# Moving the rotary and normalisation products of a random-feature attention from VectorE to GpSimd, with the three engines' head orders rotated by one head

## The reference

```python
def _softmax_kernel(x, R):
    n = jnp.sqrt(jnp.sum(x * x, axis=-1, keepdims=True))
    x = x / jnp.maximum(n, 1e-06)
    p = jnp.einsum('...d,ed->...e', x, R)
    feats = jnp.concatenate([jnp.sin(p), jnp.cos(p)], axis=-1)
    return feats / math.sqrt(F)
...
q = q * cos + _rotate_half(q) * sin
k = k * cos + _rotate_half(k) * sin
...
qp = _softmax_kernel(q, rand_matrix)
kp = _softmax_kernel(k, rand_matrix)
kv = jnp.einsum('bhsf,bhsd->bsfd', kp, v)
out = jnp.einsum('bhsf,bsfd->bhsd', qp, kv)
```

## Time and profile before

| | us |
|---|---|
| median of 3 timed runs | 7942.13 (7479.22 to 7977.28) |
| the profiled execution, own time | 7549.52 |
| its span, first to last instruction of the slowest core | 7548.1 |
| spans of the 8 cores in it | 7453.7 to 7548.1 |
| glue of stages 0 to 3 in it, with the projection under it | 388, 408, 409, 330 |
| everything after the attention stages (from 2190) | 5358 |

### The profile page before, as it was taken

One profiled execution on the slowest core, in us unless ns is written; L12 is line 12 of the kernel. 1 busy time (PEld: TensorE's weight loads), 2 busy tenths in 40 slices (PEclk: granted clock), 3 DMA queues, 4 the chain that ended last, 5 costly groups with the idle time before them and its releaser, 6 DMA issues.

```text
span 7548.1 us, 63284 instructions; the slowest of 8 cores (7453.7 to 7548.1 us)
## 1 busy us (share of the span) xinstructions
PE 5322.1 (71%) x23362; PEld 2315.3 (31%) x23362; DVE 1744.6 (23%) x2583; ACT 1411.5 (19%) x1675; POOL 561.5 (7%) x1064
## 2 busy tenths in 40 slices
PE   1364444344137599898989898539989898989891
PEld 1121111111013244343434343214434343434340
DVE  4325354454630000101010101230010101010114
ACT  4333534435341110000000000001010000000100
POOL 0000000000001011010101110001101010101010
PEclk9987677676558799999999999759999999989785
DMA  6652322323038544343434343324434343334342
GB/s 152 158 101 36 59 37 50 48 36 43 0 45 147 118 72 73 65 70 66 71 66 72 65 73 64 95 89 72 72 66 70 66 72 66 66 57 69 56 75 96
DMA packets 420666, 542.35 MB, mean 72 GB/s; under 512 B 251920, under 2 KB 268560, under 8 KB 412176
## 3 DMA queue, kind: packets, MB, share of 16 engines
q0 software_dynamic: 152640, 403.85, 32.1%
q1 hardware_dynamic: 267728, 134.46, 7.1%
HBM read 891.61 MB, written 50.33 MB: 125 GB/s over the span
## 4 chain that ended last, share of the span: by engine, by line
PE 65%; DVE 14%; ACT 10%; DMA 4%; issue 4%; SPq 2%; DVEq 1%; ACTq 0%; POOL 0%; POOLq 0%
PE pb L908 27%; PE pb L1003 27%; PE pb L591 4%; DVE nsq_b L525 4%; DVE mids L965 4%; PE pb L721 2%; ACT attn_st L654 2%; ACT L479 2%; PE pb L359 1%; DVE ot_b L1093 1%; SPq L691 1%; DMA wup_b<-wup 1%; ACT fk L491 1%; PE pb L1112 1%; SPq L666 1%
## 5 line engine op out<-in xcount | busy, mean ns | idle before, releaser
L908 PE MATMUL pb<-xn_tb,wup_b 128*128 128x512 bf16 x9216 | 2086.9, 391 | 71.3 <-DMA wup_b<-wup 71.2
L1003 PE MATMUL pb<-mids,wdn_b 128*128 128x512 bf16 x9216 | 2040.0, 385 | 110.1 <-DVE mids L965 109.3
L908 PEld LDWEIGHTS pb<-xn_tb,wup_b 128*128 128x128 bf16 x9216 | 921.6, 100 | 1235.9 <-issue 340.7
L1003 PEld LDWEIGHTS pb<-mids,wdn_b 128*128 128x128 bf16 x9216 | 912.1, 99 | 1238.1 <-issue 222.2
L965 DVE TENSOR_TENSOR mids<-mids,pb 128x4096 bf16<-128x4096 bf16 x64 | 282.9, 4421 | 2166.0 <-ACT mids L925 2159.9
L925 ACT ACTIVATE mids<-pb 128x512 bf16<-128x512 f32 x576 | 344.0, 597 | 1664.5 <-PE pb L908 1664.3
L578 PE MATMUL pb<-un_b,rt_sb 128*64 128x512 bf16 x96 | 58.1, 605 | 773.7 <-DVE un_b L529 773.7
L1025 DVE TENSOR_TENSOR acc_tb<-acc_tb,pb 128x512 f32<-128x512 f32 x320 | 219.9, 687 | 1500.2 <-PE pb L1003 1500.2
L591 PE MATMUL pb<-xn_st,wbuf 128*128 128x512 bf16 x1536 | 465.7, 473 | 55.4 <-DMA xn_st<-xn_scr 51.3
L983 POOL DMA_DIRECT2D wdn_b<-wdn x576 | 305.5, 544 | 1976.0 <-PE pb L1003 1593.7
L925 ACT ACT_TABLE_LOAD x12 | 15.4, 1283 | 2077.2 <-PE pb L908 2077.2
(11 more groups left out here) (102 smaller groups left out, 2501.5 us busy)
## 6 DMA issues: line engine op xcount, KB each, us to landing
wup_b<-wup POOLq DMA_DIRECT2D x288, 512.0 KB, 5.2
wdn_b<-wdn POOLq DMA_DIRECT2D x576, 256.0 KB, 5.0
wbuf<-wq POOLq DMA_DIRECT2D x64, 512.0 KB, 5.2
wbuf<-wo POOLq DMA_DIRECT2D x64, 512.0 KB, 6.0
x_tm<-x SPq DMA_DIRECT2D x16, 1024.0 KB, 7.7
x_tm<-xs SPq DMA_DIRECT2D x16, 1024.0 KB, 6.4
wbuf<-wk POOLq DMA_DIRECT2D x32, 512.0 KB, 5.2
wbuf<-wv POOLq DMA_DIRECT2D x32, 512.0 KB, 5.8
```

Source lines behind the costliest of these rows:

```text
L908: ins = t.matmul(pb[k % 2][:, 0:CH], wup_b[i % 2][:, kc * 128:(kc + 1) * 128], xn_tb[:, kc * TB + n * CH:kc * TB + (n + 1) * CH], start=(k ...
L1003: ins = t.matmul(pb[4 + idx % 2][:, 0:CH], wdn_b[(mc * EG + e3) % 6][:, dc * 128:(dc + 1) * 128], mids[:, e3 * DCN * TB + dc * TB + n * CH ...
```

## The change

The five bf16 products and sums of a head (L513, L515, L517, L519, L529) leave VectorE and are issued by GpSimd, on tiles of the same size and type, counted on a new semaphore `cP` (`PP = 5` for each head). VectorE keeps five instructions for a head (`NV = 5`). GpSimd's weight DMAs now stand in the same list: the first three ahead of head 0, then one behind each head's fifth instruction. Each GpSimd instruction waits for the one before it. TensorE's and ScalarE's lists are rotated: `nsq` of a head stands one round earlier relative to `phi`, and `phi` comes first in a round. Names and buffers stay as they were.

```diff
-    NV = 10
+    NV = 5
+    PP = 5
...
-        for hh in range(NHEADS + 2):
-            if hh >= 2:
-                k = hh - 2
-                t_ops.append(("nsq", k))
-                t_ops.append(("phi", k))
-                if nxt:
-                    t_ops.append(("qkv", k))
+        for hh in range(NHEADS + 3):
+            if hh >= 3:
+                t_ops.append(("phi", hh - 3))
+            if 1 <= hh <= NHEADS:
+                t_ops.append(("nsq", hh - 1))
+            if nxt and 2 <= hh < NHEADS + 2:
+                t_ops.append(("qkv", hh - 2))
             if hh < NHEADS:
                 t_ops.append(("pq", hh))
...
+            for hh in range(NHEADS):
...
+                wt(g, "G", "cS", S0 + Spos[("pqe", hh)])
+                if hh >= 4:
+                    wt(g, "G", "mT", T0 + Tpos[("nsq", hh - 4)])
+                wt(g, "G", "cP", cnt["cP"])
+                inc(g.tensor_mul(sb_[:], pq_sb[hh % 4][:], s_), "cP")
+                wt(g, "G", "cP", cnt["cP"])
+                inc(g.tensor_mul(qb[:], srcT[:, base:base + ST], c_), "cP")
+                wt(g, "G", "cP", cnt["cP"])
+                inc(g.tensor_add(qb[:], qb[:], sb_[:]), "cP")
+                wt(g, "G", "cP", cnt["cP"])
+                inc(g.tensor_mul(sb_[:], qb[:], qb[:]), "cP")
+                if hh >= 4:
+                    wt(g, "G", "mT", T0 + Tpos[("phi", hh - 4)])
+                wt(g, "G", "cV", gl_at(hh, 2))
+                wt(g, "G", "cP", cnt["cP"])
+                inc(g.tensor_mul(un_b[hh % 4][:], qb[:], invn_b[hh % 4][:]),
+                    "cP")
+                if nxt and 3 <= hh + 2 < NOC:
+                    dw(hh + 2)
...
         @blk.vector
...
             for hh in range(NHEADS):
...
-                inc(v.tensor_mul(sb_[:], pq_sb[hh % 4][:], s_), "cV")
...
-                inc(v.tensor_mul(qb[:], srcT[:, base:base + ST], c_), "cV")
...
-                inc(v.tensor_add(qb[:], qb[:], sb_[:]), "cV")
...
-                inc(v.tensor_mul(sb_[:], qb[:], qb[:]), "cV")
                 wt(v, "V", "cS", S0 + Spos[("sqrt", hh)])
                 wt(v, "V", "cV", cnt["cV"])
                 inc(v.tensor_scalar_max(nsq_b[hh % 4][:], nsq_b[hh % 4][:],
                                         1e-6), "cV")
                 wt(v, "V", "cV", cnt["cV"])
                 inc(v.reciprocal(invn_b[hh % 4][:], nsq_b[hh % 4][:]), "cV")
...
-                inc(v.tensor_mul(un_b[hh % 4][:], qb[:], invn_b[hh % 4][:]),
-                    "cV")
                 wt(v, "V", "mT", T0 + Tpos[("phi", hh)])
...
                 elif kind == "nsq":
-                    wt(t, "T", "cV", gl_at(k, 4))
+                    wt(t, "T", "cP", gp_at(k, 4))
...
                 elif kind == "phi":
-                    wt(t, "T", "cV", gl_at(k, 7))
+                    wt(t, "T", "cP", gp_at(k, 5))
```

More of the change, by code:

```diff
@@ L34 @@
 MASKV = 2.0 / 128.0
-SEM_NAMES = (["mT", "cV", "cS", "dCY", "dCG", "dsp", "dxt", "dgr", "dst",
+SEM_NAMES = (["mT", "cV", "cS", "cP", "dCY", "dCG", "dsp", "dxt", "dgr", "dst",
               "dxb", "dou", "dat", "dcc", "dwi0", "dwi1"]
@@ L412, in build_program @@
         s_ops = []
[L413 to L419, removed]
+        for hh in range(NHEADS + 3):
+            if 1 <= hh <= NHEADS:
+                s_ops.append(("sqrt", hh - 1))
+            if hh >= 3:
+                s_ops.append(("sin", hh - 3))
+            if nxt and 2 <= hh < NHEADS + 2:
+                s_ops.append(("evq", hh - 2))
             if hh < NHEADS:
@@ L426, in build_program @@
         C["Spos"] = Spos
+        C["P0"] = P0 = cnt["cP"]
         gl_at = lambda hh, k: G0 + NV * hh + k
+        gp_at = lambda hh, k: P0 + PP * hh + k
         C["glue_cV_end"] = G0 + NV * NHEADS
+        C["glue_cP_end"] = P0 + PP * NHEADS
         coV0 = G0 + NV * NHEADS
@@ L441, in build_program @@
             C["xn_ld"] = (f"dn{(st + 1) % 2}", cnt[f"dn{(st + 1) % 2}"])
[L443 to L456, removed]
+        wldn = []
@@ new lines, in build_program, with _, dw @@
+        C["wld"] = wldn
+        @blk.gpsimd
+        def _(g, st=st, nxt=nxt, T0=T0, S0=S0, Tpos=Tpos, Spos=Spos,
+              gl_at=gl_at, gp_at=gp_at, wldn=wldn):
+            c_ = cos_sb[:, st * ST:(st + 1) * ST]
+            s_ = sin_sb[:, st * ST:(st + 1) * ST]
+            def dw(j):
+                if j >= 3:
+                    wt(g, "G", "mT", qkvT_at(st + 1, j - 3))
+                else:
+                    wt(g, "G", "mT", qkvT_at(st, NOC - 1))
+                sname = f"dw{j % 3}"
+                inc(g.dma_start(out=wbuf[j % 3][:],
+                                in_=qkvsrc[j][0][qkvsrc[j][1]]), sname, 16)
+                wldn.append((sname, cnt[sname]))
+            if nxt:
+                for j in range(3):
+                    dw(j)
+            for hh in range(NHEADS):
+                isq = hh < H
+                srcT = (q_f if isq else k_f)[st % 2]
+                base = (hh if isq else hh - H) * ST
+                qb = qr_b[hh % 4]
+                sb_ = sq_b[hh % 4]
+                wt(g, "G", "cS", S0 + Spos[("pqe", hh)])
[17 more added lines that the diff above has]
+                    dw(hh + 2)
+            if nxt:
+                for j in range(NHEADS + 2, NOC):
+                    dw(j)
@@ L458, in _ @@
         @blk.scalar
         def _(s, st=st, nxt=nxt, T0=T0, S0=S0, Tpos=Tpos, Spos=Spos,
-              gl_at=gl_at, s_ops=s_ops):
+              gl_at=gl_at, gp_at=gp_at, s_ops=s_ops):
             if st >= 1:
@@ L463, in _ @@
                 wt(s, "S", "cV", caps[st - 1]["glue_cV_end"])
+                wt(s, "S", "cP", caps[st - 1]["glue_cP_end"])
             for op in s_ops:
@@ L468, in _ @@
                     if k >= 4:
-                        wt(s, "S", "cV", gl_at(k - 4, 1))
+                        wt(s, "S", "cP", gp_at(k - 4, 1))
                     wt(s, "S", "cS", cnt["cS"])
@@ L476, in _ @@
                     if k >= 4:
-                        wt(s, "S", "cV", gl_at(k - 4, 6))
+                        wt(s, "S", "cP", gp_at(k - 4, 5))
                     wt(s, "S", "cS", cnt["cS"])
@@ L500, in _ @@
         def _(v, st=st, T0=T0, S0=S0, Tpos=Tpos, Spos=Spos, gl_at=gl_at):
-            c_ = cos_sb[:, st * ST:(st + 1) * ST]
-            s_ = sin_sb[:, st * ST:(st + 1) * ST]
             for hh in range(NHEADS):
[L504 to L512, removed]
-                inc(v.tensor_mul(sb_[:], pq_sb[hh % 4][:], s_), "cV")
-                wt(v, "V", "cV", cnt["cV"])
-                inc(v.tensor_mul(qb[:], srcT[:, base:base + ST], c_), "cV")
-                wt(v, "V", "cV", cnt["cV"])
-                inc(v.tensor_add(qb[:], qb[:], sb_[:]), "cV")
-                wt(v, "V", "cV", cnt["cV"])
-                inc(v.tensor_mul(sb_[:], qb[:], qb[:]), "cV")
                 wt(v, "V", "cS", S0 + Spos[("sqrt", hh)])
@@ L525, in _ @@
                 inc(v.reciprocal(invn_b[hh % 4][:], nsq_b[hh % 4][:]), "cV")
-                if hh >= 4:
-                    wt(v, "V", "mT", T0 + Tpos[("phi", hh - 4)])
-                wt(v, "V", "cV", cnt["cV"])
-                inc(v.tensor_mul(un_b[hh % 4][:], qb[:], invn_b[hh % 4][:]),
-                    "cV")
                 wt(v, "V", "mT", T0 + Tpos[("phi", hh)])
@@ L547, in _ @@
         def _(t, st=st, nxt=nxt, T0=T0, S0=S0, Tpos=Tpos, Spos=Spos,
-              gl_at=gl_at, t_ops=t_ops, co_mT0=co_mT0, coV0=coV0, C=C):
+              gl_at=gl_at, gp_at=gp_at, t_ops=t_ops, co_mT0=co_mT0,
+              coV0=coV0, C=C):
             wt(t, "T", "dCG", cCG)
```

## The result

| | before | after |
|---|---|---|
| median, 10 timed runs each | 7777.81 (7479.22 to 7997.38) | 8077.38 (7872.62 to 8400.54) |
| profiled execution, own time | 7549.52 | 7888.15 |
| spans of its 8 cores | 7453.7 to 7548.1 | 7855.8 to 7887.1 |

The changed kernel is slower: the ratio after to before is 1.0536, 95% interval 1.047 to 1.0603.

A forecast was written before the change was run, and what follows sets the result against it. No engine is full; a head's chain handed from engine to engine bounds the attention glue. Stages 0 to 2 +315, stage 3 +13, stage ends -4 make +324 on the profiled 7549.5: 7875 us, range 7690 to 8330.

The forecast's parts named there:

- the qkv block: TensorE's matmuls (L591) between `nsq` and `pq` in stages 0 to 2, taken at 5.1 us a head.
- The ring: Closed chain from `nsq` to the next over TensorE, VectorE and GpSimd, nothing overlapping: 19.4 us a head, 14.0 in stage 3.
- its closing entry on VectorE: VectorE's list keeps the range reduction of head h ahead of maximum and reciprocal of head h+1.
- falling fast at first, so their mean is nearer the lower end: Step sizing the qkv block: five blocks in turn go from 6.28 down to 4.65 us, so 5.1 was taken.
- Rival B: TensorE's clock stays low for the whole qkv block, 6.9 us in place of 5.1: +119, total 7995; chance 0.14.
- s: Time of one of a head's five GpSimd products, gap included: taken as 1.2 us, bounded by 0.53 and 3.46.
- The ends of the stages: First heads of stages 0 and 3 lose about 4 us each, three stage ends gain 4 each: together -4 us.
- A: GpSimd nearly as quick as VectorE, s from 0.53 to 0.8 us; total 7580 at 0.53; chance 0.08.
- C: GpSimd products at s = 2.0 us, from bf16 conversion or dear completion: +352, total 8225; chance 0.13.
- D: VectorE's maximum not held behind the range reduction, so the ring avoids `phi`: 13.6 us a head, total 7470; chance 0.03.

The follow-up runs named there:

- the move alone: Kernel before, with only the five products put on GpSimd and TensorE's and ScalarE's lists unchanged: glue 1767 us (+112), lowest time 7576 us.
- the fastest kernel: Kernel before, with all three engines' lists rotated and the four rotary products on GpSimd, `un_b` staying on VectorE: ratio to before 0.9092.

## Why the prediction was right and wrong

**Right in the mechanism, wrong in two steps.** One term of the sum, the qkv block, was too small, and the sum was put on the wrong level, so that the number given said something else than the text. Both are below. The ring was read from the lists alone and is in the trace step for step: the maximum right behind the range reduction, VectorE idle for `phi`, TensorE idle for GpSimd. Undoing its closing entry on VectorE took 487 us off; taking the block out took 409 off.

**The sizes of the terms**, per head of stage 0:

| term | forecast | measured |
|---|---|---|
| `nsq` | 0.43 | 0.37 |
| qkv block | 5.1 | 6.03 |
| `pq` | 0.22 | 0.32 |
| `phi` to range reduction | 0.82 | 0.58 |
| range reduction | 2.18 | 2.19 |
| maximum and reciprocal | 3.99 | 4.08 |
| `un_b`, DMA, four products, hand-over | 6.67 | 6.90 |
| sum | 19.4 | 20.47 |

The term that was mis-sized is the block. The step that failed is "falling fast at first, so their mean is nearer the lower end": the earlier trace rows is right for the kernel before, but I carried its cycle over to a ring with 13 us of idle. There nearly all blocks are alike at 5.99. (In the kernel before the five blocks of that cycle are 6.17, 5.31, 4.87, 4.65 and 4.54 from start to start of what follows, a mean of 5.1.) Rival B had half of it: the clock is lower for most of the block, not for all of it. With 0.43 for a matmul at the lower level and 3.62 / 16 = 0.23 at the higher, 5.99 is some 12 of the 16 at the lower. The weight loads of the block shown above, one for each matmul, say the same: they come 0.43 apart as far as 653.37, and the last three stand close together.

```profile
652.94 0.15 PEld L611 LDWEIGHTS pb<-xn_st,wbuf 128*128 128x128 bf16 x1 [0.28 <-issue]
653.37 0.58 PEld L611 LDWEIGHTS pb<-xn_st,wbuf 128*128 128x128 bf16 x3 [0.28 <-issue]
```

With s at 1.29 to 1.31 instead of 1.2, the hand-over already in it, and the DMA at 0.42 instead of 0.53 the last line is 0.23 over. Over 66 intervals 1.04 more each is +69; stage 3, 14.53 for 14.0, is +12.

**The ends and the costs at nothing.** The ends of the stages came to about -1.5 us in all, where -4 was said, and by smaller terms that cancel: the first heads of stages 0 and 3 lost 1.7 and 1.6 us, not 4, and the three stage ends gave back 4.6 together, not 12. In stages 1 and 2 the first block still waits for `xn_st` (38.6 us in all on the page of the profile), which hides the slower first head. VectorE's 280 us of work taken away brought nothing, as said. "The two engines are never at work together in the ring, so I cost nothing for anything they might share" holds in the changed kernel, where none of VectorE's instructions for the 96 heads lies beside a GpSimd product, and would have failed in the move alone.

**The level.** The sum was +324, and the glue measures +404 to +406. The two profiled own times differ by 339, near the forecast, which is partly luck: the core profiled before had some 80 us in its feed-forward part that the core after had not. The step that failed here is "I keep the point at 7875 and let the range speak for that". It put a sum made on one execution (7549.5) below the median of the runs shown, 7942, so that the number reads as a kernel 0.8% faster, although the text and the chances said clearly slower, and slower it is, by 5.4%. Against the median shown, the same +324 is 8266. The measured median, 8077, lies 2.6% over the point and inside the range, and its own reference moved down to 7778 with more runs: it is 300 over that. A forecast of a ratio, 1.043 as worked out and 1.0536 measured, would have been free of this. That 8077 lies inside the range is no merit of the sum, since the range was made wide to hold this doubt among others.

**The rivals.** A: s is 1.3, far from 0.8. C: not 2.0 either. D: not in this kernel; made on purpose, its ring takes 13.83 against the 13.6 worked out, and the total 7394 against 7470.

## What to carry to other kernels

Where engines run fixed lists, write down for each instruction what stands ahead of it on its own engine as well as what it needs, and look for closed rings: rotating two lists of three made one that went through an unrelated 6 us block, and rotating the third as well was worth 487 us. A move to a slower engine costs what lies on the ring, not what the engines' busy times say: the same products were +112 in one order, +406 in another, and part of a kernel 9% faster in a third. State a forecast as a difference or a ratio first, and put it on the level of the median, not of one execution.

## What the runs showed of the hardware

- A GpSimd product of 128x512 bf16 takes 1.04 to 1.16 us and 1.29 to 1.31 from start to start where each waits for the one before, 2.5 times VectorE's 0.53. The Trainium skill's page "GPSIMD Engine Reference", section "Performance versus the Vector engine", gives about 2.6 cycles an element; at the 1.2 GHz by which the page reckons that is an estimate of 1.11 us for 512, and the trace agrees. Its measured ratio of 1.96 is for float32, and the bf16 products here do not follow it: 1.15 to 0.42 is 2.7.
- VectorE and GpSimd hold each other up, and it depends on the instruction and on who started first. When the second pass of the range reduction (float32, from SBUF to SBUF, 0.43 us) started during a GpSimd product, it ended 0.28 behind the end of that product: it took 1.38 when it started 0.06 behind the product's start (the move alone), and 0.68 when it started 0.75 behind (VectorE's list rotated). With 0.15 or less of the product left it kept its 0.43. The first and the third pass of the move alone, which read PSUM, kept 0.75 and 0.69 in all of more than 90 cases beside a product, and so did the reciprocal its 3.35 in the 84 cases of the fastest kernel. There GpSimd's products took up to 1.64 instead of 1.15, `un_b` itself up to 1.68 instead of 0.69, and some maxima 1.2. The Trainium skill's page "SBUF — State Buffer", section "Who interferes with whom", has an exclusive lock of a shared port pair: the pass that ends just behind the product is what that would give.
- The same 16 matmuls took 6.0 us where TensorE idled 13.4 us a head, 4.6 to 6.2 in a cycle of four where it idled 12.9, and mostly 3.6 in the fastest kernel, where it was busy for 101 of 153 us. The granted clock in the glue of stage 0 was 0.68 (after), 0.73 (before) and 0.91 (fastest). The idle time does not settle the length of a block: with VectorE's list rotated, heads of 13.8 us each had blocks that fell from 6.4 to 4.8 us over 18 heads and then stood at 6.4 again, while the idle time grew from 6.5 to 8. What decides it was not tried.

```profile
core 2: us, PE busy (x) PEld busy (x) DVE busy (x) ACT busy (x) POOL busy (x), PEclk, DMA share, GB/s
472.00:625.00 153.00, 101.33 (x413) 40.53 (x421) 139.49 (x125) 109.94 (x123) 122.25 (x112) 0.91 0.45 81
```

This row is of the fastest kernel. There the shorter way round paid twice: by its own terms, and by the clock that TensorE was granted.
